# Scales, shifts and the output gate of a gated-memory layer folded into per-turn factors that GpSimd makes

## What is computed

```python
q = _l2n((x @ Wq.T).reshape(Bs, Ts, Hs, Ds))
...
_, mem = jax.lax.associative_scan(comb, (a, b), axis=1)
out = _ln(mem, mn_g, mn_b) * q                  # norm over each head's 16 features
...
o = (o - m) / jnp.sqrt(var + 1e-05)             # a second norm over the same 16
o = o.reshape(Bs * Ts, Cs) * gn_g + gn_b
o = o * jax.nn.sigmoid(xc @ og_w.T + og_b)      # the output gate
return o @ Wo.T
```

## Time and profile before

| | us |
|---|---|
| median of 3 runs | 849.62 (848.96 to 851.63) |
| the profiled execution | 849.49 |
| its span | 847.5 |
| busy: PE, DVE, ACT, POOL | 742.0, 633.5, 468.4, 423.2 |

### The profile page before, as it was taken

The page is one execution under the profiler, slowest core; times in us unless marked ns, Lnnn a source line. Parts: engine busy times, 40 slices in busy tenths (PEclk is TensorE's granted clock), DMA queues, the critical chain, the costliest instruction groups (busy, mean ns, idle before and its releaser), DMA issues. The chain is left out here.

```text
span 847.5 us, 15157 instructions
## 1 busy us (share of the span) xinstructions
PE 742.0 (88%) x5602; PEld 638.1 (75%) x5602; DVE 633.5 (75%) x1099; ACT 468.4 (55%) x746; POOL 423.2 (50%) x369
## 2 busy tenths in 40 slices
PE   3368799999999999999999999999779797988773
PEld 2256678888888888888888888888567686877662
DVE  6999877788777686777778777674373998988966
ACT  4246645755655664665566565567656454664411
POOL 2344454354355667658535435436436373763831
PEclk9579999999999999999999999999889999999985
DMA  5111121111011010110100000021100000000000
GB/s 157 28 39 39 39 77 46 45 40 45 3 33 40 21 52 21 39 46 20 28 21 3 21 3 20 21 77 40 52 1 0 1 1 26 1 26 1 1 26 25
DMA packets 22108, 25.89 MB, mean 31 GB/s; under 512 B 4498, under 2 KB 17170, under 8 KB 22036
## 3 DMA queue, kind: packets, MB, share of 16 engines
q1 hardware_dynamic: 22036, 24.93, 10.4%
HBM read 14.83 MB, written 3.28 MB: 21 GB/s over the span
## 5 line engine op out<-in xcount | busy, mean ns | idle before, releaser
L652 DVE TENSOR_REDUCE neg_max<-s_pair 128x4 f32<-128x1024 f32 x127 | 155.0, 1221 | 75.5 <-PE s_pair L866 75.3
L474 ACT ACTIVATE probs<-t_pair 128x1024 f32<-128x1024 f32 x128 | 131.3, 1025 | 135.9 <-PE t_pair L891 135.6
L371 POOL TENSOR_TENSOR hid<-g,hid 128x512 f32<-128x512 f32 x64 | 82.1, 1283 | 177.7 <-DVE g L763 144.6
L365 POOL TENSOR_TENSOR hid_lo<-hid,hid_hi 128x512 fp32r<-128x512 f32 x64 | 85.5, 1336 | 82.7 <-ACT hid_hi L497 82.6
L866 PE MATMUL s_pair<-K,Q 96*128 96x256 f32 x508 | 84.8, 290 | 16.1 <-DVE neg_max L652 9.8
L866 PEld LDWEIGHTS s_pair<-K,Q 96*128 96x128 f32 x508 | 75.5, 194 | 24.5 <-issue 8.1
L891 PE MATMUL t_pair<-Q,K 104*128 104x512 f32 x256 | 85.6, 416 | 0.3 <-DMA Q<-max_parts 0.3
L933 PE MATMUL down<-hi,hid_hi 128*128 128x256 f32 x256 | 83.9, 328 | 0.8 <-POOL hid_lo L365 0.8
L906 PE MATMUL misc<-probs,V 128*32 128x256 f32 x1024 | 69.4, 389 | 4.0 <-DVE kc L608 2.5
L933 PE MATMUL down<-lo,hid_hi 128*128 128x256 f32 x256 | 71.5, 279 | 0.0
L933 PE MATMUL down<-hi,hid_lo 128*128 128x256 f32 x256 | 71.2, 278 | 0.0
(11 more groups left out here) (258 smaller groups left out, 1962.9 us busy)
## 6 DMA issues: line engine op xcount, KB each, us to landing
stage<-in_ternary SPq DMA_DIRECT2D x18, 256.0 KB, 2.8
Q<-q_hi SPq DMA_DIRECT2D x64, 64.0 KB, 2.0
stage<-in_scales SPq DMA_DIRECT2D x8, 384.0 KB, 3.3
X<-in_x SPq DMA_DIRECT2D x8, 256.0 KB, 4.4
Q<-q_lo SPq DMA_DIRECT2D x32, 64.0 KB, 2.0
Q<-max_parts SPq DMA_DIRECT2D x128, 4.0 KB
out<-X SPq DMA_DIRECT2D x8, 256.0 KB, 2.3
signs<-w_stage SPq DMA_DIRECT2D x9, 128.0 KB, 1.8
```

Source lines behind the costliest of these rows:

```text
L365: pool.tensor_tensor(hid_lo[:, m % 2, :, :].rearrange("p a n -> p (a n)"), hid[:, m % 2, :], hid_hi[:, m % 2, :, :].rearrange("p a n -> p ...
L371: pool.tensor_tensor(hid[:, m % 2, :], g[:, m % 2, :], hid[:, m % 2, :], ALU.mult).then_inc(S["hid_done"], 1)
L474: act.activation(probs[:, u % 2, th, :], t_pair[:], ACT.Exp, scale=SCALE).then_inc(S["probs_done"], 1)
L652: dve.tensor_reduce(neg_max[:, u % 2, 4 * jp:4 * jp + 4], score_banks(u, jp)[:].rearrange("p (s n) -> p s n", n=SEQ), AX_X, ALU.max, negat ...
```

## The change

The algebra is regrouped. Queries times `mn_b` goes to `o`, queries times `mn_g` back to `q_kept` (`queries_weighted`, 4 operations on GpSimd); the product of the centred memory with the weighted queries is made on VectorE ahead of the root (in `memory_summed`), and behind the root stand a product and a sum for each half. In the same way gate times `gn_b` goes to `q_kept` and gate times `gn_g` back to `gates` (`gates_weighted`, 4 operations on GpSimd, once `q_kept` has been read), the centred output is multiplied by the weighted gate on GpSimd (`output_weighted`), and behind the second root stand a product and a sum for each half on VectorE. `queries_kept` moves behind `output_high` on ScalarE, and in the last turn `mlp_added` behind `output_applied`.

```diff
+                def queries_weighted():
+                    wait("q_kept", 1)
+                    wait("o_turned", 0)
...
+                    for b in range(BPG):
+                        inc(pool.tensor_tensor(heads(o[:, pair(b), :]), heads(q_kept[:, pair(b), :]), mn_b, ALU.mult), "mq_done")
+                    for b in range(BPG):
+                        wait("mq_done", b + 1)
+                        inc(pool.tensor_tensor(heads(q_kept[:, pair(b), :]), heads(q_kept[:, pair(b), :]), mn_g, ALU.mult), "mq_done")
...
+                def gates_weighted():
+                    wait("mw_done", BPG)
+                    wait("gates_done", TPG)
+                    for b in range(BPG):
+                        inc(pool.tensor_tensor(q_kept[:, pair(b), :], gates[:, 1 + late % 2, pair(b), :], gn_b2, ALU.mult), "gw_done")
+                    for b in range(BPG):
+                        g = gates[:, 1 + late % 2, pair(b), :]
+                        wait("gw_done", b + 1)
+                        inc(pool.tensor_tensor(g, g, gn_g2, ALU.mult), "gw_done")
...
+                def output_weighted(b):
+                    wait("cen_sq", b + 1)
+                    wait("gw_done", BPG + b + 1)
+                    inc(pool.tensor_tensor(o[:, pair(b), :], o[:, pair(b), :], gates[:, 1 + late % 2, pair(b), :], ALU.mult), "xg_done")
...
@@ GpSimd's turn
-                memory_scaled(pool, late, 1)
+                queries_weighted()
+                gates_weighted()
...
+                output_weighted(0)
+                if early is not None:
                     hidden_low(pool, early, 3)
+                output_weighted(1)
...
-                gated(pool, late, 0)
@@ ScalarE's turn
-                    queries_kept()
                     hidden_high(5)
                 for b in halves:
                     output_high(b)
+                if early is not None:
+                    queries_kept()
@@ VectorE, memory_summed
                         inc(dve.tensor_reduce(sm[:, b, :], osq[:, b, :].rearrange("p (h d) -> p h d", d=L1_DH), AX_X, ALU.add), "sm_done")
+                        wait("mq_done", BPG + b + 1)
+                        y = turned(banks[4 + b][:])
+                        inc(dve.tensor_tensor(y, y, q_kept[:, pair(b), :], ALU.mult), "mw_done")
@@ VectorE, memory_normed
-                        inc(dve.tensor_tensor(heads(o[:, pair(b), :] if b else y), heads(y), each(sm[:, b, :]), ALU.mult), "mn_done")
+                        inc(dve.tensor_tensor(heads(y), heads(y), each(sm[:, b, :]), ALU.mult), "mn_done")
+                    for b in range(BPG):
+                        wait("mn_done", b + 1)
+                        inc(dve.tensor_tensor(o[:, pair(b), :], turned(banks[4 + b][:]), o[:, pair(b), :], ALU.add), f"op_done{b}")
@@ VectorE, output_applied
+                        wait("xg_done", b + 1)
                         inc(dve.tensor_tensor(heads(y), heads(o[:, pair(b), :]), each(s2[:, b, :]), ALU.mult), "on_done")
+                    for n, b in enumerate(halves):
+                        wait("on_done", n + 1)
+                        inc(dve.tensor_tensor(o[:, pair(b), :], turned(banks[4 + b][:]), q_kept[:, pair(b), :], ALU.add), f"o_done{b}")
@@ VectorE's turn
-                memory_scaled(dve, late, 0)
...
-                gated(dve, late, 1)
```

More of the change, by code:

```diff
@@ L1157, in through_input_gate @@
             inc(engine.tensor_tensor(vn[:, pair(b), :], qk[:, 1, pair(b), :], gates[:, 0, pair(b), :], ALU.mult), f"b_done{b}")
[L1159 to L1176, removed]
         @block.sync
@@ L1230, in convolved @@
                         inc(pool.tensor_tensor(xc_lo[:, k, :], cs[:, k, :], xc_hi[:, k, :].bitcast(F32), ALU.subtract), "xc_lo_done")
+                def queries_weighted():
+                    wait = waiter(pool, late)
+                    wait("q_kept", 1)
+                    wait("o_turned", 0)
+                    if late == 0:
+                        pool.wait_ge(once["scaled"], 4)
+                    for b in range(BPG):
[4 more added lines that the diff above has]
+                def gates_weighted():
+                    wait = waiter(pool, late)
+                    wait("mw_done", BPG)
[7 more added lines that the diff above has]
+                def output_weighted(b):
+                    wait = waiter(pool, late)
+                    wait("cen_sq", b + 1)
+                    wait("gw_done", BPG + b + 1)
+                    inc(pool.tensor_tensor(o[:, pair(b), :], o[:, pair(b), :], gates[:, 1 + late % 2, pair(b), :], ALU.mult), "xg_done")
                 if late is None:
@@ L1366, in queries_kept @@
                     wait("norm_done", 1)
-                    wait("op_done0", 0)
-                    wait("op_done1", 0)
+                    wait("o_done0", 0)
+                    wait("o_done1", 0)
                     wait("ro_done", 0)
@@ L1610, in output_normed @@
                     wait("q_kept", 1)
-                    wait("mlp_done", 1)
+                    if early is not None:
+                        wait("mlp_done", BPG)
                     squared, root = (banks[4][:, n * BPG * PAIR_HEADS:(n + 1) * BPG * PAIR_HEADS] for n in range(2))
@@ L1622, in output_applied @@
                     wait("ro_done", 1)
-                    for b in range(BPG):
-                        y = turned(banks[5][:]) if b else o[:, pair(b), :]
+                    for b in halves:
+                        y = turned(banks[4 + b][:])
+                        wait("xg_done", b + 1)
                         inc(dve.tensor_tensor(heads(y), heads(o[:, pair(b), :]), each(s2[:, b, :]), ALU.mult), "on_done")
+                    for n, b in enumerate(halves):
+                        wait("on_done", n + 1)
+                        inc(dve.tensor_tensor(o[:, pair(b), :], turned(banks[4 + b][:]), q_kept[:, pair(b), :], ALU.add), f"o_done{b}")
                 def output_low(b):
@@ L1684, in turn @@
                 output_summed()
-                if early is None:
-                    mlp_added(0)
-                    mlp_added(1)
                 output_normed()
@@ L1691, in turn @@
                 output_applied()
-                gated(dve, late, 1)
                 if early is not None:
                     hidden(5)
+                else:
+                    mlp_added(0)
+                    mlp_added(1)
                 for b in halves:
@@ L1775, in ffn_down @@
                     if early is not None:
-                        if b == 0:
-                            wait("op_done0", 1)
-                        wait("mn_done", b + 1)
+                        wait(f"op_done{b}", 1)
                     for t in range(2 * b, 2 * b + 2):
```

7 lines of the change are left out of this document (3 added, 4 removed).

## The result

| | before | after |
|---|---|---|
| median, us | 849.29 (4 runs, 848.85 to 851.63) | 860.25 (4 runs, 858.30 to 861.14) |
| ratio | | 1.0124, 95% interval 1.0103 to 1.0146 |
| span of the profiled execution | 847.5 | 859.2 |

The account below looks back on a forecast made before the run. Waits between nearly full VectorE and TensorE bound each turn, with GpSimd's linked operations at its end. Turn terms 4.0 + 5.2 + 0.2 + 1.0 = 10.4 on the profiled 849.49 gave 860 us, range 853 to 864.

Parts of the forecast that it names:

- the terms of the second and fourth turn: Predicted net loss per turn: second +5.2 us (3.05 to the turn's end, 2.2 behind), fourth +1.0 (-4.1 without holds).
- that of the third: Third turn: 2.65 us lost at ffn_up(2), 4.46 idle available, 1.1 to hidden(5) and hidden_high(5), 0.9 to held steps: +0.2.
- (b): First root beside gates_weighted: VectorE's SBUF-only steps held, one let through per GpSimd operation; stall 4.0 us.
- (a): Head of the second turn: two VectorE products ahead of hidden(0) make it and ffn_up(1) 1.2 us later.
- (c): Between first root and hidden(1): four VectorE operations instead of two, 1.2 us more; ffn_up(2) then starts 4.4 later.
- (d): Second turn's end: output_weighted holds second root's steps 1 to 2 us; TensorE's 1.34 idle is gained, leaving +3.05.
- (e): Turn's tail: queries_kept now delays first_tap, and GpSimd work holds VectorE's convolution steps: +2.2 us until the residual, second turn.
- The clock as a rival: TensorE's idles lower its granted clock: later matmuls 1.5 us slower, two or three times not hidden; 863 to 865, chance 0.12.

Follow-up runs that it names:

- x1: Kernel before, with four added GpSimd products (results not used) that begin beside the first root: 860.31 us, ratio 1.0119.
- e1: Kernel after, with GpSimd's gates_weighted starting only when the first root is done: 852.64 us, ratio 1.0030.
- e5: Kernel after, with the first root's intermediate y in a PSUM bank instead of SBUF, in the last turn alone: 856.74 us, ratio 1.0079.
- e2: Kernel after, with the two products behind hidden(0) instead of ahead of it: 869.25 us, ratio 1.0229.
- e9: e6 without the wait of gates_weighted for the first root: 862.12 us, ratio 1.0155.
- e8: e6 with the two products ahead of hidden(0) again: 851.00 us, ratio 1.0029.
- x3: Kernel before, with hidden(0) ahead of the two reductions and nothing else changed: 845.88 us, ratio 0.9951.
- e7: e6 with hidden(0) ahead of the two reductions as well: 843.71 us, ratio 0.9936.
- e6: Kernel after: gates_weighted waits for first root, products behind hidden(0), gate x shift in own buffer, queries_kept back, queries x mn_b behind convolution: 844.92 us, ratio 0.9944.

## Why the prediction was right

The time, the mechanism and the place were as forecast. That the sum fits so closely owes something to luck: the terms of the second and fourth turn were each some 0.45 too high, that of the third 0.9 too low. Point by point:

- **(b), the root.** Forecast 6.2 us with steps of 1.1 to 1.3; measured 5.95, 5.95, 5.93 and 6.31, with three steps of 1.20 to 1.23 and a first one of 0.9; in the fourth turn the first step is short (0.18) and the next four take 1.18 to 1.29. One step passed for each GpSimd operation, as read off two rows. x1 shows that the hold is enough for a loss of this size, e1 that it is the greatest part here, e5 that for a two-input step it hangs on both inputs being in SBUF. The Trainium skill, SBUF — State Buffer, Who interferes with whom, has the exclusion last for the whole instruction. The rows speak for a border that is a little earlier: L1602 ended at 725.21 and needs 0.19, so it began at 725.02, while GpSimd's first operation, half of the pair of 723.89, ended at 723.89 + 1.27 = 725.16. That is 0.14 before the recorded end, as in the earlier trace rows.
- **(a) and (c).** Forecast: `ffn_up(2)` 4.65, 4.4 and 2.65 later in the first three turns. Measured from scan to `ffn_up(2)`: 4.5, 4.0 and 2.4. In the second turn TensorE idled 3.90 before `ffn_up(1)` (forecast 3.6) and 1.03 before `ffn_up(2)` (1 to 3). In the first turn the convolution steps lost 2.0 (forecast 1.95).
- **(d).** In the second turn `ffn_up(2)` to the turning shrank by 1.2 (forecast 1.3). The second root lost 0.9, less than the 1 to 2 forecast, and still without effect.
- **(e).** From the turning to the next scan 8.12 in place of 6.19, +1.93 (forecast 2.2); in the first turn 8.10 in place of 7.40, +0.7 as forecast.
- **Turns.** +4.1, +4.8, +1.1, +0.6, against +4.0, +5.2, +0.2, +1.0: the sum of 10.4 is 10.5. The term that was mis-sized is the third turn. To the turning it was right (+2.4 and -2.2 against +2.65 and -2.5). Behind it 0.93 came for which the prediction has no term. The output's low part reached TensorE 3.06 us behind the start of the turning, where it had been 2.52. ScalarE's `hidden_high(5)`, released by `hidden(5)` (VectorE, 816.12), now runs directly ahead of `output_high`, which begins 1.71 behind the start of the turning and not 1.15. The prediction put 1.1 in for these two, but counted it up to the turning alone. The other 0.4 lies in the output product, where the stretch at the lower clock now covers nearly all of its matmuls (5.0 us from first to last, before 4.65). Another 1.2 us of the span's difference lies ahead of the first turn's scan. That stretch took 658.7 to 660.2 us in the kernels built on the one before and 657.0 to 662.4 in those built on the one after, so I take it for scatter. The third turn's rows (turning, `hidden_high(5)` and `output_high`, then the first of the output product):

```profile
815.66 1.25 PE L1855 MATMUL lbank<-ident,rows 128*128 128x128 f32 x8 [2.15 <-DVE rows L1650]
816.83 0.63 ACT L1355 ACTIVATE hi<-l_hid 128x512 fp32r<-128x512 f32 x1 [2.69 <-DVE l_hid L1570]
817.37 1.07 ACT L1411 ACTIVATE o_hi<-lbank 128x512 fp32r<-128x512 f32 x2
818.72 0.79 PE L1734 MATMUL lbank<-lo,o_hi 128*128 128x256 f32 x2 [1.81 <-DVE o_lo L1655]
```

- **The clock as a rival.** The stretch at 1.2 GHz came where it was looked for, on `ffn_up(1)` of the second turn (3.58 instead of 2.12), and was hidden there. In the first and third turn it was there before the change too (3.55 and 3.64, now 3.73 and 3.49), which the prediction did not see. e2 and e9 show the other case.

The forecast was right about the change, less so about what stands behind it. x1 shows that I had read the slack at the wrong engine: for this change the reading did no harm, since here TensorE did come to wait at `ffn_up(2)`, for 1.03. e2, e8 and x3 missed their expectations, by the rows because I priced every shift as if TensorE's clock would stay.

## What to carry to other kernels

Before work moves to GpSimd, list what VectorE does beside it. Here a short VectorE step with both inputs in SBUF, 0.23 us long, took 1.2 beside a GpSimd operation that reads SBUF, and a chain of dependent ones paid that again at each of four operations. Two remedies worked: let the chain finish first (e1), or put one operand in PSUM (e5). Slack has to be read on the engine that is delayed, up to its own next pause (0.42 on VectorE here, not 2.2 on TensorE). When an idle of TensorE moves, look at the granted clock behind its new place: in e2 eight matmuls there took 3.78 us instead of 2.12. And hold single turns, not only totals, against each other: the output product took 2.8 or 4.3 us by the clock that it met, and that alone moved 1.2 us from one turn to the other in x1 and x3.

## What the runs showed that was not expected

- GpSimd operations that only write (ten of 128x512 in 4.83 us) don't hold VectorE's two-input steps (0.23), but hold one-input steps between SBUF tiles (0.19 to between 0.58 and 1.04, 0.20 to 0.48).
- The same eight matmuls took 2.1 us after idles of 1.0 to 1.6, and 3.1 to 3.8 after idles of 3.2 to 6.5, in every run. In between both came: 2.12 after 2.41, 2.53 after 2.03 (e7, first turn), 3.40 after 2.69 (e6), 2.15 after 2.90 (e1, third turn), 3.78 after 2.88 (e9). And in e2 they took 3.41 with no idle directly before. The idle just before doesn't decide alone.
- Moving one VectorE product ahead of two reductions gave 3.9 us in the kernel before (x3), where 0.4 a turn was expected from VectorE's wait. TensorE's idle before `ffn_up(1)` went from 3.25, 2.41 and 2.69 us to 2.03, 1.53 and 1.20.
